# Attention values and denominators as one column-tiled group late in a unit, denominators inverted as 128 by 16 by way of small transfers

## The reference, cut to what matters

```python
k = concatenate([null_k, compress(k)]); v = concatenate([null_v, compress(v)])   # 1 + 512 keys for 2048 queries
dots = einsum('bhid,bhjd->bhij', q, k) * d ** (-0.5)
dots = where(q_idx[:, None] < k_idx[None, :], mask_value, dots)                   # causal, null key always seen
attn = softmax(dots, axis=-1)
out = einsum('bhij,bhjd->bhid', attn, v)
...
shared = silu(xf @ sh_gate_w) * (xf @ sh_up_w) @ sh_down_w
```

## Time and profile before

| what | value |
|---|---|
| median of 3 runs (lowest, highest) | 5419.1 us (5416.88, 5422.39) |
| span of the profiled execution | 5418.5 us |
| mean granted TensorE clock | 0.992 |
| busy, of the span | PE 98%, PEld 82%, DVE 71%, POOL 56%, ACT 48% |

### The profile page before, as it was taken

How to read it: one execution, slowest core, us unless ns; L and a number is a source line. 1 busy time by engine, 2 the same in 40 slices (tenths; PEclk the granted TensorE clock), 3 DMA queues, 4 the chain that set the end, 5 groups by cost and what they waited for, 6 DMA issues and landing times. The chain is left out here.

```text
span 5418.5 us, 102292 instructions
## 1 busy us (share of the span) xinstructions
PE 5303.0 (98%) x32880; PEld 4440.9 (82%) x32880; DVE 3828.9 (71%) x7311; ACT 2615.1 (48%) x3833; POOL 3028.9 (56%) x2716
## 2 busy tenths in 40 slices
PE   8999989999999999998999999999999999999999
PEld 6888866766666667667999999989999999999786
DVE  6666667778787877775676666766667666666664
ACT  3333333333343333335666666666666666666410
POOL 1222215666666665115777777777777777777514
PEclk9999989999999999998999999999999999999999
DMA  7777764444454444435676677767787676676748
GB/s 239 248 242 255 250 173 129 133 134 119 136 148 135 119 141 118 134 98 119 134 158 112 134 170 150 163 132 167 158 227 158 135 164 129 134 156 113 178 154 289
DMA packets 500414, 864.75 MB, mean 160 GB/s; under 512 B 64388, under 2 KB 165493, under 8 KB 497694
## 3 DMA queue, kind: packets, MB, share of 16 engines
q1 hardware_dynamic: 356014, 567.12, 33.2%
q0 software_dynamic: 140928, 292.13, 29.5%
q10 hardware_dynamic: 3312, 3.47, 0.3%
HBM read 498.49 MB, written 330.47 MB: 153 GB/s over the span
## 5 line engine op out<-in xcount | busy, mean ns | idle before, releaser
L1754 POOL DMA_INDIRECT mid_base<-e_rows,e_ox x556 | 1160.3, 2087 | 372.5 <-POOL e_ox L1749 239.5
L1865 DVE TENSOR_TENSOR e_wgu_lo<-e_wgu,e_wgu_hi 128x2048 fp32r<-128x2048 f32 x278 | 637.5, 2293 | 806.4 <-ACT e_wgu_hi L1788 676.6
L1742 POOL DMA_INDIRECT e_xg<-mid_xn,e_ix x556 | 625.5, 1125 | 336.4 <-POOL e_ix L1739 226.4
L1801 ACT CAST e_xT_hi<-e_ps_t 128x512 fp32r<-128x512 f32 x556 | 299.1, 590 | 929.8 <-PE e_ps_t L1931 929.8
L1069 POOL DMA_INDIRECT mid_ids<-b_pairs,b_cell x512 | 614.3, 1200 | 141.8 <-issue 141.0
L1944 PE MATMUL e_ps_g<-e_xT_hi,e_wgu_hi 128*128 128x256 f32 x2224 | 652.9, 294 | 1.7 <-issue 1.7
L1944 PE MATMUL e_ps_g<-e_xT_lo,e_wgu_hi 128*128 128x256 f32 x2224 | 630.0, 283 | 0.0
L1944 PE MATMUL e_ps_g<-e_xT_hi,e_wgu_lo 128*128 128x256 f32 x2224 | 629.7, 283 | 0.0
L1944 PE MATMUL e_ps_u<-e_xT_hi,e_wgu_hi 128*128 128x256 f32 x2224 | 629.4, 283 | 0.0
L1944 PE MATMUL e_ps_u<-e_xT_lo,e_wgu_hi 128*128 128x256 f32 x2224 | 629.4, 283 | 0.0
L1944 PE MATMUL e_ps_u<-e_xT_hi,e_wgu_lo 128*128 128x256 f32 x2224 | 629.4, 283 | 0.0
(11 more groups left out here) (286 smaller groups left out, 13368.0 us busy)
## 6 DMA issues: line engine op xcount, KB each, us to landing
b_xT_hi<-mid_xT_hi SPq DMA_DIRECT2D x32, 1024.0 KB
b_xT_lo<-mid_xT_lo SPq DMA_DIRECT2D x32, 1024.0 KB
mid_base<-b_x SPq DMA_DIRECT2D x32, 1024.0 KB
e_wgu<-in_gate_w SPq DMA_DIRECT2D x62, 512.0 KB
e_wgu<-in_up_w SPq DMA_DIRECT2D x62, 512.0 KB
e_wd<-in_down_w SPq DMA_DIRECT2D x62, 512.0 KB
ec_cell<-mid_base SPq DMA_DIRECT2D x88, 256.0 KB, 4.9
ab_q<-mid_q_hi SPq DMA_DIRECT2D x82, 256.0 KB, 4.0
```

The lines of the kernel that those rows point to most:

```text
L1742: pool.indirect_dma_start(xg[s][:, i, :], None, t["xn"], bass.IndirectOffsetOnAxis(ap=ix[s][:, i:i + 1], axis=0))\
L1754: pool.indirect_dma_start(t[f"base{i}"], bass.IndirectOffsetOnAxis(ap=ox[s][:, i:i + 1], axis=0), rows[s][:, i, :], None, compute_op=ALU.a ...
L1801: act.copy(xT_hi[s][:, i * DC // 2 * RB:(i + 1) * DC // 2 * RB], ps_t[i][:, :]).then_inc(xT_hi_ready, 1)
L1865: dve.tensor_tensor(wgu_lo[s][:, :], wgu[s][:, :], wgu_hi[s][:, :].bitcast(F32), ALU.subtract)\
```

## The change

Values and denominators move together. A table `TILED` says for each n in which slot which key tiles' values are made; the denominators follow directly behind the last of them. With n = 3 there are two groups, in slot 6 and at the end of slot 0 of the next unit (`SLOTS`).

The inversion takes another road. ScalarE issues a transfer that turns one row of `den` for each head (4 × 512) into `den16` (128 × 16); VectorE inverts that in one instruction; ScalarE stores it to a DRAM buffer `rden` (4 × 512) and spreads it from there to 32 rows for each head (`rden`, 128 × 512, 256 KB). `finish` multiplies by that. `normalise` moves from slot 1 to slot 2.

```diff
+        TILED = {0: {7: [0]}, 1: {9: [1, 0]}, 2: {11: [2, 0, 1]}, 3: {6: [3, 0], SLOTS: [1, 2]}}
+
         def pv_slots(n, k):
-            if k == 6:
-                return [n]
-            return [kt for kt in range(n) if 7 + 2 * kt == k]
+            return TILED[n].get(k, [])
...
             def finish(u):
-                pool.wait_ge(rden_ready, QTC * (u + 1))
+                pool.wait_ge(rden_in, 16 * (u + 1))
...
-                pool.tensor_tensor(att[u % 2][:, :], o[:, :], den[:, :], ALU.mult).then_inc(att_ready, 1)
+                pool.tensor_tensor(att[u % 2][:, :], o[:, :], rden[:, :], ALU.mult).then_inc(att_ready, 1)
...
+            def turn_den(u):
+
+                act.wait_ge(den_ready, u + 1)
+                act.dma_start(den16[:, :], den[0:P:DH, :].rearrange("h (j c) -> h j c", j=DH)).then_inc(den16_in, 16)
+
+            def store_rden(u):
+                act.wait_ge(den16_ready, u + 1)
+                act.dma_start(t["rden"].rearrange("h (j c) -> (h j) c", j=DH), den16[:, :]).then_inc(rden_out, 16)
+
+            def spread_rden(u):
+                act.wait_ge(rden_out, 16 * (u + 1))
+                if u:
+                    act.wait_ge(att_ready, u)
+                act.dma_start(rden[:, :], t["rden"][:, None, :].broadcast_to([HPC, DH, QC])).then_inc(rden_in, 16)
...
+                    if u and k == 3:
+                        turn_den(u - 1)
+                    if u and k == 7:
+                        store_rden(u - 1)
+                    if u and k == 9:
+                        spread_rden(u - 1)
...
-            def invert(u, i):
-                dve.wait_ge(den_ready, u + 1)
-                part = den[:, i * P:(i + 1) * P]
-                dve.reciprocal(part, part).then_inc(rden_ready, 1)
+            def invert(u):
+                dve.wait_ge(den16_in, 16 * (u + 1))
+                dve.reciprocal(den16[:, :], den16[:, :]).then_inc(den16_ready, 1)
...
-                    if k == 1 and u:
+                    if k == 2 and u:
                         normalise(u - 1)
-                    if 2 <= k < QTC + 2 and u:
-                        invert(u - 1, k - 2)
+                    if k == 6 and u:
+                        invert(u - 1)
...
+            def tiled(u, k):
+                n = u % NCH
+                for kt in pv_slots(n, k):
+                    values(u, kt)
+                if k == max(TILED[n]):
+                    denominators(u)
...
-                    for kt in pv_slots(n, k):
-                        values(u, kt)
-                    if k == 7 and n == 0:
-                        denominators(u)
-                    if k == 0 and u and (u - 1) % NCH:
-                        denominators(u - 1)
+                    if k == 0 and u:
+                        tiled(u - 1, SLOTS)
+                    tiled(u, k)
```

More of the change, by code:

```diff
@@ L776, in stage_b @@
         den = sb("den", [P, QC])
+        den16 = sb("den16", [P, QC // DH])
+        rden = sb("rden", [P, QC])
         o = sb("o", [P, QC])
@@ L837, in stage_b @@
         od_emptied = sem("od_emptied")
-        rden_ready = sem("rden_ready")
+        den16_in = sem("den16_in")
+        den16_ready = sem("den16_ready")
+        rden_out = sem("rden_out")
+        rden_in = sem("rden_in")
         att_ready = sem("att_ready")
@@ L1177, in _ @@
                         null_exponent(u)
+            turn_den(NU - 1)
+            store_rden(NU - 1)
+            spread_rden(NU - 1)
         @block.vector
@@ L1232, in normalise @@
                     dve.wait_ge(att_ready, u)
+                    dve.wait_ge(den16_in, 16 * u)
                 dve.tensor_tensor(den[:, :], ps_d[:, :], p_null[:, :], ALU.add).then_inc(den_ready, 1)
@@ L1401, in _ @@
             normalise(NU - 1)
-            for i in range(QTC):
-                invert(NU - 1, i)
+            invert(NU - 1)
         @block.tensor
@@ L1544, in _ @@
                         scores_null(u)
-            denominators(NU - 1)
+            tiled(NU - 1, SLOTS)
 class Ahead:
@@ L2322, in internal @@
         cnt=d("cnt", (P, EXPERTS)), ids=d("ids", (NSLOT, 2), I32), blk=d("blk", (1, 3 * P), I32), used=d("used", (1, 3), I32),
-        attT=d("attT", (DC, P, TOK)), passed=nc.alloc_semaphore("passed"))
+        attT=d("attT", (DC, P, TOK)), rden=d("rden", (HPC, QC)), passed=nc.alloc_semaphore("passed"))
 def layout(L0_attn_x, L0_attn_Wqkv, L0_attn_conv_w, L0_attn_conv_b, L0_attn_null_k, L0_attn_null_v, L0_attn_W_out,
```

## The result

The changed kernel takes 5754.0 us (median of 4 runs, 5747.4 to 5759.7) against 5418.0 for the kernel before: 1.0619 of its time, 95% interval 1.0604 to 1.0634. The profiled execution spans 5751.9 us. The forecast was 5652 us, with a range up to 5745: the direction was right, the size was too small by 102 us, and the time lies 9 us above the range.

What follows compares the result with a forecast made beforehand. TensorE was taken to bound the attention stage, busy 495 of 500 us. On 5418.5 us: tiling −46, reciprocals −15, xT waits +217, clock +72, end of stage +4.5, giving 5652 us, range 5535 to 5745.

Steps and rivals of the forecast that it cites:

- The part on tiling: TensorE's values and denominators groups: 9 fewer separate groups per round, 0.32 us each, gain 46 us, at least 29.
- The waits for xT: TensorE at the start of even units: new waits of 3.5 us (n = 1) and 11.0 (n = 3), 15 each, 217 us.
- The clock: TensorE's granted clock at 0.50 behind each new wait: 2.4 us lost for each of 30, 72 us.
- a little under half: Reciprocals leaving VectorE shorten TensorE's waits for row maxima: 15 us gain, between nothing and 38.
- The turn's cover: Slots 4 and 5, about 2.1 us each, in which the turn of the denominators (2.0 us) can land before VectorE inverts.
- Not later than before: Turning and inverting the denominators would be done no later than the old inversion; no cost in the sum.
- The end of the stage: The last unit's inversion is exposed, with its transfers, at the end of the attention stage: +4.5 us.
- The late result holds up nothing: Rival: xT still arrives in time behind SP's store, only the gains remain, 5362 us; chance 0.06.
- Only n = 3 stalls: Rival: the xT wait after n = 1 units vanishes, leaving the one after n = 3, 5563 us; chance 0.08.
- GpSimd's masks become the wait: Rival: the late multiplication also delays GpSimd's masks and the values of slot 6 in n = 3, 5677 us; chance 0.06.

Runs made afterwards that it cites:

- e1: The changed kernel with SP's store of the attention result issued last in each unit, behind the loads of x and xT: 5536.0 us (ratio 1.0216).
- e12: The kernel before the change, with SP's store of the attention result issued last in each unit, as a control: 5418.9 us (0.9999).
- e2: The changed kernel's grouping of values and denominators with the old inversion (four reciprocals on VectorE, no small transfers): 5479.1 us (1.0110).
- e6: e5 with the first two values groups of n = 1 and n = 2 joined in slot 7, where VectorE adds: 5381.1 us (0.9932).
- e8: e2 with VectorE's additions of n = 1 and n = 2 moved behind the evictions, the n = 1 group moved to slot 11: 5378.5 us (0.9932).
- e9: The changed kernel with VectorE's additions and the n = 1 group placed as in e8, SP's order unchanged: 5712.3 us (1.0541).
- e4: The changed kernel with SP's load of q in even units issued behind the store of x: 5756.0 us (1.0626).
- e11: The changed kernel with e5's SP order, e8's additions, and the next item's keys and values also loaded behind the turn: 5344.9 us (0.9872).
- e5: e1 with SP also waiting for the turned denominators to land before it issues the loads of x and xT: 5465.9 us (1.0095).

## Where the prediction was right, and which steps of it failed

**The mechanism held.** The result is late by two transfers, SP stands at its store, xT behind it comes late, TensorE stops at the start of every even unit, and half clock follows. e1 and e12 together show it: the same move of the store takes all xT waits out of the changed kernel and changes nothing in the kernel before.

**The step that failed: moved groups were costed by their length alone.** The part on tiling took 0.32 us for each joined group and did not ask what the group had left, so the slot 8 waits stood in the sum at nothing. The groups of slots 6 and 7 were TensorE's work during VectorE's first addition. What the prediction did not name is the queue on VectorE: behind the addition stand the evictions of slot 7. e2, e6 and e8 show it from three sides (no late result needed, a group put back, the addition moved away). Of the miss of 102 us this is 42 (changed kernel less e9); without it the time would have been e9's 5712, inside the range.

**The waits for xT were mis-sized.** In e9, where they stand alone, they come to 291 us, and the forecast had 217. At n = 3 the chain has 5.05 for the spread (4.1) and 8.5 for xT (7.3): the median landing of xT_lo is 8.9, and it is 0.8 less in e4, where the loads of q do not follow at once. At n = 1 the store was shorter than I took (1.41 to the issue of the spread, against 2.0), the spread longer (5.29 from issue to multiplication) and xT again (8.9 from issue to TensorE); there lay no slack to take it up, so that 3.5 became about 6 (6.43 in unit 21 to 22 of e9). In e9 the 15 larger waits come to 193 us (12.8 each, forecast 11.0) and the 16 smaller ones to 99 (6.2 each, forecast 15 of 3.5); the one of the first round, which the forecast left out, came too, with 6.6 us. Together this is 74 us of the miss. By the Trainium skill (DMA: Bandwidth & Descriptors, "Anatomy of one DMA — SWDGE (gpsimd) path") an estimate for the spread, from a fixed 2.0 us and 436 GB/s fitted on GpSimd's issues, is 2.6 us. The trace shows 5.05 and 5.29, about twice that, up to the start of its reader. The nearest row was the better guide, though still too low.

**The clock was sized well**: 72 us for 30 waits. In e9, what lies above e11 and is no wait for xT is 5712 − 291 − 5345 = 76 us, as 31 waits of 2.45; other effects of the late result are in that too. The granted clock of e9, counted as above, gives 69 us, 2.2 for each wait.

**The gains were right in sum, wrong in parts.** Joined groups alone brought 39.5 us (e8 against before; forecast 46, lower bound 29), 0.27 per group. The new inversion without its collisions brought 34 (e8 to e11), the longer end of the stage already paid, where I had 15 less 4.5; without the end (6.1) it is 40, at the bound of 38. e8 still waits at weight loads for VectorE's row maxima (760 to 2400 us), where e11 has 7.0 us:

```profile
PEld b_ps_s L1438 <- DVE b_mx L1218: 53.6, 156, 1.0
```

So nearly all of those waits went, not "a little under half". That the reciprocals alone made them is argued: from e8 to e11 SP's order and the loads of keys and values move as well, and only SP's store has a control (e12). All of the gains with the end come to 73 us (e11 against before) where the forecast had 46 + 15 − 4.5 = 56.5, so 16.5 us of the miss go the other way: 42 for slot 8, 74 for xT, 4 for the clock, less 16.5, are 104, against 102. That these add up is no proof of them, for the clock's term is what is left between e9 and e11; the xT waits and the granted clock are read from the traces by themselves.

**The turn's cover.** "Not later than before" was right for the changed kernel (VectorE held once, 3.2 us), but only because xT and x came late themselves. Once they were in time, the cover was gone (e1).

**The end of the stage** was taken as 4.5 us longer. The longest wait for the gathered rows of the next stage, 25.6 us before, is 31.7 after: 6.1.

**The rivals.** "The late result holds up nothing" is ruled out by the 234 us. "Only n = 3 stalls" too: n = 1 does, and by more than forecast. "GpSimd's masks become the wait" did not come: no wait of TensorE names the masks, in e9 to e11 neither.

## What to carry to other kernels

Before moving a piece of work off an engine's row, ask what waited behind its back: the same microseconds may have covered another engine's long instruction, and the group's length says nothing about that. A queue that waits in order turns one late result into late loads for something unrelated, so put the store of a result that may come late behind the loads that must not. When such a queue is freed, look at what its large loads now meet: an 8 KB transfer that others wait for should be ahead of megabytes, by a wait if need be (e5 against e1, 70 us).

## What the runs showed of the hardware that was not expected

A pause of TensorE of 1.9 us was followed, in the stretch shown, by 3.3 us at a granted clock of 0.50 (1.2 GHz) while it was busy throughout; another of 2.2 us was not followed by any. e2 against e8 puts the cost at some 37 us for 34 such pauses, the granted clock at 46. A transfer of 8 KB issued just after 2 MB from another engine's queue took 7.3 us to reach its reader, and in e5, where that load waits for it, 15 units instead of 46 are held by it. A 256 KB spread from DRAM took 5.0 to 5.3 us from issue until GpSimd went on, more than the 4.1 of a load of the same size in the kernel before.
